# A decoder layer with a mixture of experts: the order of VectorE's tile step, and who loads half of the first weights

## What is computed

```python
x = _layernorm(x + self_attention(x))                       # 16 heads of 64, causal
x = _layernorm(x + cross_attention(x, ctx_1024, mask))      # 16 heads of 16
# two groups of 32 experts; each token takes its 2 best experts of each group
logits = x2 @ router_w; scores = softmax(logits)
w, e = top_k(scores, 2)
y = (silu(x2 @ wg[e]) * (x2 @ wu[e])) @ wd[e]               # 256 -> 128 -> 256, times w, summed over the 2
out = (out0 * 2 + out1 * 2) / 4
x = _layernorm(x + out)
```

## Time and profile before

| | |
|---|---|
| median of 3 runs | 4887.19 us (4886.07 to 4888.65) |
| the profiled execution | 4894.84 us, span of its profile 4893.1 us |
| first block | 0 to about 3750 us |
| second block | about 3750 to 4893 us |
| PE busy | 4755.2 us, 97% |
| DVE busy | 3782.2 us, 77% |
| ACT busy | 3412.7 us, 70% |
| POOL busy | 2712.7 us, 55% |
| DMA | 556.18 MB, mean 114 GB/s; 255 to 299 GB/s in most of the second block |

### The profile page before, as it was taken

The page is one execution under the profiler, slowest core; times in us unless marked ns, Lnnn a source line. Parts: engine busy times, 40 slices in busy tenths (PEclk is TensorE's granted clock), DMA queues, the critical chain, the costliest instruction groups (busy, mean ns, idle before and its releaser), DMA issues. The chain is left out here.

```text
span 4893.1 us, 133371 instructions
## 1 busy us (share of the span) xinstructions
PE 4755.2 (97%) x38848; PEld 3976.5 (81%) x38848; DVE 3782.2 (77%) x18828; ACT 3412.7 (70%) x13380; POOL 2712.7 (55%) x3750
## 2 busy tenths in 40 slices
PE   7999999999999999999999999999995999999998
PEld 6888888888888888888888888888874766676665
DVE  4888888888888888888888888888883455547777
ACT  5788888878878888887887888788783444444443
POOL 3455555555555555555555555555554555556666
PEclk9999999999999999999999999999997999999999
DMA  4121111112112111211211211121125799878888
GB/s 137 62 69 61 58 65 64 57 60 69 58 58 67 62 58 64 65 58 57 67 62 57 67 64 58 61 67 58 58 78 162 255 299 298 273 246 270 273 273 255
DMA packets 477157, 556.18 MB, mean 114 GB/s; under 512 B 55602, under 2 KB 407860, under 8 KB 475956
## 3 DMA queue, kind: packets, MB, share of 16 engines
q1 hardware_dynamic: 350516, 300.08, 19.9%
q0 software_dynamic: 52224, 146.87, 8.0%
q10 hardware_dynamic: 73728, 100.70, 6.8%
HBM read 270.08 MB, written 277.35 MB: 112 GB/s over the span
## 5 line engine op out<-in xcount | busy, mean ns | idle before, releaser
L527 POOL TENSOR_TENSOR yTl<-yT,yTh 128x256 fp32r<-128x256 f32 x512 | 381.7, 745 | 910.7 <-DVE yTh L979 907.6
L756 ACT ACTIVATE prob<-prob,negmax 128x128 f32<-128x128 f32 x2048 | 799.0, 395 | 102.5 <-DVE negmax L827 98.3
L1155 POOL DMA_INDIRECT y_d<-y,to x576 | 593.2, 1030 | 464.6 <-DVE y L1290 447.8
L756 ACT ACTIVATE xprob<-xprob,xnegmax 128x128 f32<-128x128 f32 x2048 | 792.9, 392 | 1.6 <-DVE xnegmax L827 1.6
L1208 PE MATMUL bank<-moe,xgT 128*128 x2304 | 594.6, 381 | 0.0
L589 POOL DMA_INDIRECT xs_d<-xrow,place x512 | 515.9, 1008 | 128.1 <-issue 128.1
L1290 DVE COPY y<-bank 128x256 f32<-128x256 f32 x576 | 244.5, 424 | 407.4 <-PE bank L1224 290.0
L827 DVE CUSTOM_DVE_ANT_0 prob<-bank,causal 128x128 f32<-128x128 f32 x2048 | 471.7, 286 | 34.0 <-PE bank L695 20.9
L774 ACT COPY probT<-bank 128x512 f32<-128x512 f32 x512 | 300.0, 586 | 248.0 <-PE bank L705 181.1
L827 DVE CUSTOM_DVE_ANT_0 xprob<-bank,xmask 128x128 f32<-128x128 f32 x2048 | 470.5, 286 | 1.2 <-remote 1.2
L837 DVE TENSOR_TENSOR prob<-prob,inv 128x512 f32<-128x512 f32 x512 | 438.9, 857 | 20.2
(11 more groups left out here) (180 smaller groups left out, 14188.3 us busy)
## 6 DMA issues: line engine op xcount, KB each, us to landing
xg<-xs_d SPq DMA_DIRECT2D x576, 136.0 KB
xs_d<-blank SPq DMA_DIRECT2D x248, 272.0 KB
rows<-y_d ACTq DMA_DIRECT2D x256, 256.0 KB
xT_s<-xT SPq DMA_DIRECT2D x128, 128.0 KB
x<-x SPq DMA_DIRECT2D x128, 128.0 KB, 2.0
cT<-cT SPq DMA_DIRECT2D x128, 128.0 KB
x_d<-x SPq DMA_DIRECT2D x128, 128.0 KB, 2.0
sums<-x_d ACTq DMA_DIRECT2D x128, 128.0 KB
```

Source lines behind the costliest of these rows:

```text
L527: nc.gpsimd.tensor_tensor(yT_p[1][:, c, :], yT[:, c, :], yT_p[0][:, c, :].bitcast(F32), ALU.subtract).then_inc(y_split, 1)
L756: last = nc.scalar.activation(dst[:, h, :], dst[:, h, :], ACT.Exp, bias=src_bias[:, h:h + 1], scale=-1.0, accum_out=acc[:, h:h + 1])
L1155: nc.gpsimd.indirect_dma_start(y_d[:, :], bass.IndirectOffsetOnAxis(ap=to[:, m % NTO:m % NTO + 1].bitcast(U32), axis=0), y_s[q][:, :], Non ...
```

## The change

Four things are changed. VectorE makes `to` and h at the beginning of its step instead of behind y and the second sum. The second half of the first weights is issued by ScalarE at the beginning of the second block, after the owners are read, and no longer by SyncE at the end of the first. On GpSimd the token rows of the last batch (127) are made after the scatters of batch 126 and no longer before its blocks are opened. And the tiles `xg_s` hold, and are loaded with, 258 instead of 272 values a row.

```diff
                     pipeline(sp, iteration)
                     sp.wait_ge(cleared, CLEAR * clears_for(NB - 1))
-                    sp.wait_ge(mixed, NB * NG)
-                    first_half(sp, 1)
...
-                            if s == 1 and t.live(4):
+                            if s == 1 and t.live(4) and t.item(4) < NB - 1:
                                 token_rows(t.item(4))
                             if s == 2 and t.live(4):
                                 open_blocks(t.item(4))
                             if t.live(5):
                                 scatter(t.item(5), s)
+                            if s == 3 and t.item(4) == NB - 1:
+                                token_rows(t.item(4))
...
-            xg_s = [sb(f"xg{q}", [P, ROW]) for q in range(NX)]
+            xg_s = [sb(f"xg{q}", [P, D + 2]) for q in range(NX)]
...
-                            sp.dma_start(xg_s[q][:, :], xs_d[g][(n - g * TILES) * P:(n - g * TILES + 1) * P, :]).then_inc(xg_in[q], 16)
+                            sp.dma_start(xg_s[q][:, :], xs_d[g][(n - g * TILES) * P:(n - g * TILES + 1) * P, 0:D + 2]).then_inc(xg_in[q], 16)
...
                 @block.scalar
                 def _(act):
+                    act.wait_ge(owners_in, 16 * NGRP)
+                    first_half(act, 1)
+
                     def iteration(t, n):
...
                     def iteration(t, n):
+                        if t.live(1):
+                            q, m = t.slot(1), t.item(1)
+                            dve.wait_ge(gate_in, m + 1)
+                            wait(dve, ht_made, t.item(2))
+                            v.tensor_tensor(to[:, m % NTO:m % NTO + 1], xg_s[m % NX][:, CODE:CODE + 1], spare_no[:, m % SPARE:m % SPARE + 1],
+                                            ALU.max).then_inc(to_made, 1)
+                            v.tensor_tensor(h_s[q % 2][:, :], gate_s[q % 2][:, :], GB[q % 2][:, HID:2 * HID], ALU.mult).then_inc(h_in, 1)
                         now = combined(n - COMBINE)
...
                             v.scalar_tensor_tensor(s[:, :], rows[:, k % NR, 1, :], weight_of(g, b, 1), s[:, :], ALU.mult, ALU.add).then_inc(sum_ready, 1)
-                        if t.live(1):
...
```

## The result

The median went from 4887.92 us to 4765.06 (4764.59 to 4770.77), a ratio of 0.9751 with a 95% interval of 0.9739 to 0.9762. The span of the profiled execution went from 4893.1 to 4763.7 us; its time, 4765.47, lies at the median, while the one before, 4894.84, lay 6.9 above its median, so the sum in spans (-129.4) is about 7 larger than that in medians.

What follows compares the result with a forecast made beforehand. The expert stage was taken to be bound by TensorE waiting for h, made late behind y and a sum on VectorE, plus the seam between blocks. Terms -89 + 5 + 0 - 4.5 + 13.5 = -75 gave 4812 us, range 4788 to 4858.

Steps and rivals of the forecast that it cites:

- Part 1: Expert stage: making h first on VectorE takes steps beside combinations from 1.95 to 1.775 us, 500 steps, -89 us.
- Part 2: Weight bursts in the expert stage: the same bytes in 9% less time can make transfers late, +5 us (0 to 20).
- feared y ring: Four y tiles between VectorE's copy and GpSimd's send: 6.6 us from copy to next copy, against 7.10 available.
- Part 3: Loads of xg: rows of 1032 instead of 1088 bytes, 1.3% of DMA load, off the path, 0 us.
- Part 4: Seam between the blocks: last token rows no longer wait for batch 125's scatters on GpSimd, -4.5 us.
- Part 5: Start of second block: ten weight issues hold ScalarE 17 us ahead of its first xgT copy, +13.5 us.
- The signs: Profile after: h-load idle near 60 us, 505 records per 100 us, second block near 3745.4, ten issues 15 us or more.
- The slower cases: Expert stage: y ring bounds part of the gain, 4836 to 4860 us (0.16), or takes over wholly, 4896 to 4946 (0.07).
- That h was not the cause: Expert stage: the 0.50 us stall is TensorE's own register work; only the seam is left, 4896 us, chance 0.05.
- rival 2: Expert stage: y landing in 6.5 us makes steps 1.83 us; 4836 us, up to 4860 at 6.8, chance 0.16.
- All five rivals: Forecast 4812 us (0.62), ring partly 4836 (0.16), short ScalarE issues 4800 (0.10), ring wholly 4896 (0.07), h not cause 4896 (0.05).

Runs made afterwards that it cites:

- h first alone: The kernel before with places and h moved to the beginning of VectorE's step, nothing else: 4759.69 us, ratio 0.9733 (0.9718 to 0.9748).

## Why the prediction came out as it did

**Part 1, the step that failed.** "Four steps without a late h are 4 x 1.68 and 0.38 for the table read" was right of the kernel before and was then used as the floor of the kernel after, with "the change leaves that alone" said of the read. Both halves were wrong: a step without a read is 1.63 when h is early, and the read adds 0.03 us, 0.11 or 0.27 by the stretch, not 0.38. By the sizes: 250 steps in group 0 went from 1.948 to 1.651, 250 in group 1 from 1.952 to 1.711, and 76 without combinations from 1.765 to 1.622, which is 74 + 60 + 11 = 145 us where 89 were taken and 100 was the end. The forecast had counted the 0.37 us by which h would be early as cover against stalls, worth nothing in itself. The time of h itself was right (+0.57 forecast, +0.60 measured); what was wrong was that TensorE wanted it at +0.94, a time that h itself had set. The load now comes at +0.87 with h 0.27 early, and the sequencer need not stand at that wait: the steps without a read drop from 1.68 to 1.63, the table read all but vanishes where nothing is combined, and shrinks beside combinations. The hint lay beside the earlier trace rows: in the step called clean, h started at 3801.80 and ended at 3802.08, and its load came at 3802.14. So it did in all but one of the tiles without a read. An operand that arrives just in time everywhere is a bound, even with no idle time before its user. With h put back to +0.89 the kernel took 4812.49, so the mechanism as predicted, a late h removed in 250 steps, was right as far as it went. That 4812.49 so nearly meets the forecast's 4812 is luck in part: the profiled execution, for which the forecast had 4820, took 4813.62.

**Part 2** was forecast at +5. The windows give 145 and the stage as a whole 135, so bursts, start and drain together took about 10, inside the 20 of its range. In the burst from 3880 to 3900 the records fall to 94, and TensorE waits 6.6 us for xg in four places over the stage; that load was not among the suspects. The feared y ring shows (25.1 us of waits in 53 places, the longest 1.5), and costs little, as the h of its step stands ahead of it; waits for an h that came late, most of them behind such a wait, are 8.2 us, part of them already in the windows of the 145. How the 10 us divide was not traced piece by piece. The load of the DMA engines was near the forecast: 319 and 308 GB/s beside combinations where 305 was expected, and 383 in the burst of 3860 to 3880, where "over 400" was.

**Part 3**, 0: as measured.

**Part 4** was forecast at -4.5 and came to -5.1, the right size for partly the wrong reason. The sentence that the leaving of SyncE's issue "saves only what Part 4 has" fell: it shortens the wait for landings by itself (5.21 to 1.52 us), and late rows without it save only 2.3.

**Part 5** was forecast as a hold of 17 us and a delay of 13.5. The kernel after, the end of the owners' load from the chain and ScalarE's timeline:

```profile
3744.07 3.35 DMA rows<-xs_d
```

```profile
3747.44 1.07 ACTq L203 DMA_DIRECT2D moe<-g  x2
3748.54 4.32 ACTq L203 DMA_DIRECT2D moe<-u  x2
3752.89 4.01 ACTq L203 DMA_DIRECT2D moe<-g  x2
3756.93 2.95 ACTq L203 DMA_DIRECT2D moe<-u  x2
3759.91 3.13 ACTq L206 DMA_DIRECT2D moe<-d  x2
3763.08 0.65 ACT L1239 COPY xgT<-bank 128x256 f32<-128x256 f32 x2 [43.41 <-DMA moe<-d]
```

The owners are in at 3747.42, and the ten issues end at 3763.04. The hold is 15.6 us, the copy comes 15.66 after the owners instead of 3.5: +12.2. The releaser named in the last row is not what held the copy; the five rows above it are. The Trainium skill's page "DMA: Bandwidth & Descriptors" says in "Issuing engines are not separate DMA queues" that an issuer's own time is usually small relative to the DMA; the measurement decides here against that for a burst of this size, as it did for SyncE.

**The signs.** Held: the block's start (3743.44 for 3745.4), the last scatter some 8 us before it, the length of the ten issues, the first copy. Missed: "one in four" steps stays long at 2.08 (the steps with a read are 1.66, 1.74 and 1.92 in the three stretches), 505 records in 100 us (545 and 526), near 60 us of idle time before the h load (40.9). y copies waiting for their send had been named as a sign of a wrong forecast; they came, and they were not the reason. VectorE in group 1, 89% full (88.55 of 100 us), stayed under the 95% that had been named as another.

**The rivals.** The slower cases asked for a ring that bounds the step; it appeared with 25 us of waits, most of them hidden. That h was not the cause is excluded by h first alone. (By its own formula, rival 2 with a landing of 6.8 us is 4873 and not 4860.) All five rivals shared one floor of 1.775 us, so none could reach 4765; the range's lower end, 4788, was built on the same number.

## What to carry to other kernels

A step measured while an operand arrives just in time is not the engine's floor: before a floor is taken from "clean" steps, look whether the operand's end and its use are a few hundredths apart in them too, and if so, keep a case in which the steps get shorter. Moving the producer of an in-order engine's next operand to the front of its own engine's program can also hide part of that engine's register reads, which look fixed before. A burst of large DMA issues belongs on a queue with nothing urgent behind it, and beside work whose own transfers have slack.

## What the runs showed of the hardware

- A table read by TensorE lengthened its step by 0.35 to 0.40 us where h came 0.05 us before its load and nothing was combined. With h 0.27 us early and one read in four steps it added 0.03 us there, 0.11 in group 0 and 0.27 in group 1; with one read in two steps, 0.18 where nothing is combined.
- The read's own record was 486 to 512 ns in the first case and 298 to 307 in the second (3800 to 3830).
- Ten issues of 6.3 MB held whoever made them for about the same time: SyncE 15.0 us before and 16.1 in the second block, ScalarE 15.6. On ScalarE the first two took 1.07 us in all, the later ones 1.4 to 2.5 each.
- The same load, issued beside the last scatters, lengthened the wait for their landing from 7.28 to 10.06 and 10.25 us.
- 5% fewer bytes in a row of xg (1032 instead of 1088) made no difference that can be told (ratio 1.0013, 0.9996 to 1.0031).
